# Node-number rows made behind the dst-ordered loop of a graph-network kernel, with table rows on ScalarE and clearing stores on three queues

## What is computed

```python
# layer 0: row = src, col = dst
msg_1 = x @ W_m1.T + b_m1
msg_2 = x @ W_m2.T + b_m2
msg_e = edge_attr @ W_me.T + b_me
msg = relu(msg_1[row] + msg_2[col] + msg_e)
msg = relu(msg @ W_net.T + b_net)
agg = segment_max(msg, row, num_segments=N_NODES)
agg = where(isfinite(agg), agg, 0.0)
x = layernorm(x + x @ W_o1.T + b_o1 + (agg @ W_o2.T + b_o2))
# layer 1
message = mlp2(concat(x[src], x[dst]))
aggregated = segment_sum(message, dst, num_segments=N_NODES)
x = layernorm(x + x + mlp2(concat(x, aggregated)))
```

## Time and profile before

| what | us |
| --- | --- |
| median of 3 runs | 2929.59 |
| the 3 runs | 2926.2, 2930.57, 2929.59 |
| time of the profiled execution | 2931.22 |
| its span | 2929.5 |
| mean granted TensorE clock | 0.942 of full |
| preparation block and sort test | 0 to 174.3 |
| dst-ordered loop block | 174.3 to 1274.6 |
| src-ordered loop block | 1274.6 to 1770.5 |
| node update, second edge loop, output | 1770.5 to 2929.5 |
| busy in the span: TensorE, VectorE, ScalarE, GpSimd | 2376.6, 2027.2, 1025.1, 1903.4 |

### The profile page before, as it was taken

How to read it: one execution, slowest core, us unless ns; L and a number is a source line. 1 busy time by engine, 2 the same in 40 slices (tenths; PEclk the granted TensorE clock), 3 DMA queues, 4 the chain that set the end, 5 groups by cost and what they waited for, 6 DMA issues and landing times. The chain is left out here.

```text
span 2929.5 us, 92861 instructions
## 1 busy us (share of the span) xinstructions
PE 2376.6 (81%) x22750; PEld 2069.7 (71%) x22751; DVE 2027.2 (69%) x10493; ACT 1025.1 (35%) x2315; POOL 1903.4 (65%) x2609
## 2 busy tenths in 40 slices
PE   7857777666677677759999998688888889898997
PEld 6546666555566566647777775588888888898987
DVE  7868988888888888747878776544454555555556
ACT  6324433333333333324444446322222222222225
POOL 1027777777777777754444446677777777777774
PEclk9778988999988989879999999999999999999998
DMA  5112222222222222248898883222222222222221
GB/s 181 40 39 48 47 47 47 47 47 47 47 46 47 47 46 47 65 133 226 226 226 227 226 224 81 52 53 52 52 52 52 52 52 52 52 52 52 52 50 45
DMA packets 603553, 240.09 MB, mean 82 GB/s; under 512 B 533568, under 2 KB 574300, under 8 KB 603228
## 3 DMA queue, kind: packets, MB, share of 16 engines
q1 hardware_dynamic: 439104, 96.80, 16.7%
q0 software_dynamic: 53216, 94.66, 11.6%
q10 hardware_dynamic: 111164, 47.81, 5.8%
HBM read 143.61 MB, written 101.41 MB: 84 GB/s over the span
## 5 line engine op out<-in xcount | busy, mean ns | idle before, releaser
L1000 POOL DMA_INDIRECT edge_in_src_order<-u,place x832 | 808.2, 971 | 275.8 <-issue 212.3
L1555 POOL DMA_INDIRECT a_rows<-src_table,idx x782 | 751.8, 961 | 255.4 <-issue 238.0
L1654 ACT ACTIVATE h<-ps_h 128x512 f32<-128x512 f32 x208 | 124.2, 597 | 773.4 <-PE ps_h L1626 699.7
L1159 PE MATMUL ps_u<-we_s,attrT 128*128 128x384 f32 x416 | 194.6, 551 | 246.8 <-ACT u L1187 246.0
L1254 POOL COPY m_s<-m 128x144 f32 x832 | 233.8, 326 | 245.1 <-PE ps_pre L1301 244.3
L1599 DVE TENSOR_SCALAR ohd_f<-iota_b,dloc_c 128x128 f32<-128x128 bf16 x832 | 184.0, 289 | 280.6 <-PE ps_n L1636 280.4
L1635 PE MATMUL ps_s<-ohd_f,h 128*128 128x128 f32 x1664 | 359.2, 305 | 0.0
L1588 DVE TENSOR_TENSOR hsumT<-hsumT,ps_s 128x128 f32 x832 | 239.0, 287 | 158.3 <-issue 69.9
L1621 PE MATMUL ps_h<-a_rows,ident 128*128 x1664 | 240.6, 288 | 126.2 <-SPq L1564 125.4
L1277 DVE TENSOR_TENSOR_SCAN top<-same,top,ps_net 96x512 f32<-96x512 bf16 x207 | 264.1, 1276 | 98.0 <-PE ps_net L1308 97.7
L1187 ACT COPY u<-ps_u 128x384 f32<-128x384 f32 x208 | 99.7, 479 | 587.8 <-DMA edge_in_src_order<-u,place 564.1
(11 more groups left out here) (309 smaller groups left out, 5497.4 us busy)
## 6 DMA issues: line engine op xcount, KB each, us to landing
u_in<-edge_in_src_order SPq DMA_DIRECT2D x208, 192.0 KB, 3.4
running_max<-row ACTq DMA_DIRECT2D x208, 192.0 KB, 4.1
rowt<-src_row SPq DMA_DIRECT2D x208, 130.0 KB, 3.7
key_in<-edge_keys SPq DMA_DIRECT2D x832, 2.0 KB
attr_in<-edge_attributes SPq DMA_DIRECT2D x832, 8.0 KB
edge_in_src_order<-u,place POOLq DMA_INDIRECT x832
a_rows<-src_table,idx POOLq DMA_INDIRECT x782
edge_attributes<-in_edge_attr ACTq DMA_DIRECT2D x8, 784.0 KB, 12.4
```

What stands on the lines that cost most here:

```text
L1000: pool.indirect_dma_start(u_d, bass.IndirectOffsetOnAxis(place[:, u, j:j + 1], 0), ur[:, u, j, :], None).then_inc(sent[u], 16)
L1159: m.matmul(ps_u.rearrange("p j f -> p (j f)"), attrT[:, u, :], we_s[:].rearrange("p j f -> p (j f)"), start=True, stop=False, skip_group_c ...
L1555: pool.indirect_dma_start(a_rows[:, 4 * u + j, :], None, a_d, bass.IndirectOffsetOnAxis(idx[:, u % 4, j:j + 1], 0)).then_inc(got[u % 4], 16)
```

## The change

In the preparation block:
- the 8 attribute copies move from ScalarE's queue to SP's, behind a wait for the x loads and ahead of the 51 zero stores
- the ten table instructions L556 to L561 (five for each half) move from VectorE to ScalarE, as `activation` with `Copy`; TensorE waits for `rows_read` where it waited for VectorE
- the marks, the sums and the store of the node-number rows are taken out; eight small counts are kept in `begun`, and `at_f`, `iota_w`, `one_w` and `tri` live on
- of the 49 zero stores by block, SP keeps 16, ScalarE's queue gets 16, and 17 move to GpSimd's queue at the start of the next block

In the dst-ordered block:
- GpSimd issues its 17 zero stores, waits for all 49, and only then begins to send
- the attribute loads of groups 0 to 3 are issued by ScalarE's queue, their key loads by SP's
- the output weights are loaded by SP behind its loop, and GpSimd adds the identity to one of them behind its sends
- the marks, sums, rows and their store stand behind the loop on TensorE and VectorE, ahead of the tail

```diff
 # preparation, SP
+                        sp.wait_ge(xt_in, 16 * NT)
+                        part = EP // 8
+                        for c in range(8):
+                            sp.dma_start(attr_d[part * c:part * c + part, :], edge_attr[part * c:part * c + part, :]).then_inc(attr_out, 16)
                         sp.wait_ge(consts, ALL_CONSTS)
...
-                        for b in range(0, NB, 4):
+                        for b in range(0, 16, 4):
...
-                        sp.wait_ge(rows_set, 8)
...
+                        sp.wait_ge(attr_out, 16 * 8)
                         sp.wait_ge(key_out, 16)
 # preparation, ScalarE
-                        act.wait_ge(xt_in, 16 * NT)
...
+                        def row(to, of, scale, bias):
+                            return s.activation(to, of, ACT.Copy, scale=float(scale), bias=float(bias))
+                        for h in range(2):
+                            part = slice(h * HN, (h + 1) * HN)
+                            act.wait_ge(to_dve, 3 + 2 * h)
+                            row(e0_row[:, part], ps_b[0:1, 0:HN], KEY, E * KEY).then_inc(rows_read, 1)
+                            act.wait_ge(to_dve, 4 + 2 * h)
+                            row(db_row[:, part], ps_c[0:1, 0:HN], 1, -1)
...
+                            row(off_s[:, part], ps_c[:, 0:HN], P, -P).then_inc(rows_read, 1)
+                        act.wait_ge(zeros_out, 16 * (NS - FULL + 2))
+                        act.wait_ge(pads_ready, 1)
+                        slots = u_d.rearrange("e f -> (e f)")
+                        for b in range(16, 32, 4):
+                            at = offsets(nc, mybir.EngineType.Activation, pl_row[0:1, b:b + 4], (POS - P) * F)
...
 # preparation, TensorE
-                                pe.wait_ge(to_pe, 5)
+                                pe.wait_ge(rows_read, 2)
...
 # dst-ordered block, SP
+                            if isinstance(i, int) and i < 4:
+                                return
...
                         pipeline(sp, G, [(0, load)])
+                        for to, of in ((wo1_s[:], wo1), (wo2_s[0:F, :], wo2), (wo2_s[F:F + 2, :], bo),
...
+                        sp.wait_ge(rows_set, 8)
 # dst-ordered block, GpSimd
-                        pool.wait_ge(node_w_in, 16 * 6)
...
+                        for b in range(32, NB, 4):
+                            at = offsets(nc, mybir.EngineType.Pool, pl_row[0:1, b:min(b + 4, NB)], (POS - P) * F)
+                            for j in range(min(4, NB - b)):
+                                nc.gpsimd.dma_start(slots[bass.ds(at[j], P * F)].rearrange("(p f) -> p f", f=F), zero_rows[:]).then_inc(rest_set, 16)
+                        pool.wait_ge(pads_set, 16 * 32)
+                        pool.wait_ge(rest_set, 16 * (NB - 32))
+                        pipeline(pool, G, [(0, send)])
+                        pool.wait_ge(node_w_in, 16 * 6)
...
 # dst-ordered block, VectorE, behind the loop and ahead of the tail
+                        for b in range(NB):
+                            wait(dve, marked, b - 3)
+                            v.tensor_scalar(oh_group[:, b % 4, :], iota_w[:, 0:G], at_f[:, 0, b:b + 1], None, ALU.is_equal)
+                            v.tensor_scalar(oh_slot[:, b % 4, :], iota_w[:], at_f[:, 1, b:b + 1], None, ALU.is_equal).then_inc(marks_set, 1)
...
 # dst-ordered block, TensorE, behind the loop
+                        pe.wait_ge(place_chain, 4 * G)
+                        for b in range(NB):
+                            pe.wait_ge(marks_set, b + 1)
...
 # dst-ordered block, ScalarE
+                        act.wait_ge(ones_set, 2)
+                        for i in range(4):
+                            at = offsets(nc, mybir.EngineType.Activation, e0_row[0:1, 4 * i:4 * i + 4], E * KEY)
+                            for j in range(4):
+                                act.dma_start(attr[:, i, j, 1:1 + KA], attrs[bass.ds(at[j] * (KA // KEY), P * KA)].rearrange("(p w) -> p w", w=KA)).then_inc(rec_in[i], 16)
                         pipeline(act, G, [(4, rows), (1, turned)])
```

More of the change, by code:

```diff
@@ L187, in gnn @@
         upto_f = sb(whole, "upto_f", [P, CG])
+        tri = sb(whole, "tri", [P, P])
+        iota_w = sb(whole, "iota_w", [P, 512], F16)
+        at_f = sb(whole, "at_f", [P, 2, HB])
+        one_w = sb(whole, "one_w", [P, 512])
+        begun = sb(whole, "begun", [P, 2, 4])
         e0_row = sb(whole, "e0_row", [1, NS], I32)
@@ L462, in _ @@
                             act.dma_start(we_s[W * j + 1:W * j + 1 + KA, j, :], w_e).then_inc(rows_in, 16)
-                        act.wait_ge(xt_in, 16 * NT)
-                        part = EP // 8
-                        for c in range(8):
-                            act.dma_start(attr_d[part * c:part * c + part, :], edge_attr[part * c:part * c + part, :]).then_inc(attr_out, 16)
                         for b in range(NT):
@@ L548, in _ @@
                         groups(LATE + 8, LATE + 13)
-                        for h in range(2):
-                            if h == 1:
-                                groups(LATE + 13, LATE + 16)
-                            part = slice(h * HN, (h + 1) * HN)
-                            dve.wait_ge(to_dve, 3 + 2 * h)
-                            v.tensor_scalar(e0_row[:, part], ps_b[0:1, 0:HN], float(E), float(KEY), ALU.add, ALU.mult).then_inc(to_pe, 1)
-                            dve.wait_ge(to_dve, 4 + 2 * h)
-                            v.tensor_scalar(db_row[:, part], ps_c[0:1, 0:HN], -1.0, None, ALU.add)
-                            v.tensor_scalar(df_row[:, part], ps_c[0:1, 0:HN], float(F), -float(F), ALU.mult, ALU.add)
-                            v.tensor_scalar(dd_row[:, part], ps_c[0:1, 0:HN], float(D), -float(D), ALU.mult, ALU.add)
-                            v.tensor_scalar(off_s[:, part], ps_c[:, 0:HN], float(P), -float(P), ALU.mult, ALU.add).then_inc(to_pe, 1)
+                        groups(LATE + 13, LATE + 16)
                         groups(LATE + 16, Q8)
@@ L889, in _ @@
                             pe.wait_ge(totals, 1)
-                            m.matmul(ps_first[:, 0:1], tri[:], cum[:, P - 1:P], start=True, stop=True).then_inc(firsts, 1)
+                            m.matmul(ps_first[:, 0:1], tri_s[:], cum[:, P - 1:P], start=True, stop=True).then_inc(firsts, 1)
                             def rank(q, u, n):
@@ L1166, in _ @@
                         pipeline(pe, G, [(2, equal), (1, turn), (3, product), (3, count)])
+                        pe.wait_ge(place_chain, 4 * G)
+                        for b in range(NB):
+                            pe.wait_ge(marks_set, b + 1)
+                            for q, (lo, hi) in enumerate(halves):
+                                mm = m.matmul(ps_mark[q][0:hi - lo, :], oh_group[:, b % 4, lo:hi], oh_slot[:, b % 4, :],
+                                              start=(b == 0), stop=(b == NB - 1), skip_group_check=True)
+                            mm.then_inc(marked, 1)
+                        pe.wait_ge(passed_set, 2)
+                        rest_n = G - P
+                        m.matmul(ps_ahead[:, 0:1], tri[:], passed_c[:, 0, 511:512], start=True, stop=True)
+                        m.matmul(ps_ahead[0:rest_n, 1:2], onesf[:, 0:rest_n], passed_c[:, 0, 511:512], start=True, stop=False)
+                        m.matmul(ps_ahead[0:rest_n, 1:2], tri[0:rest_n, 0:rest_n], passed_c[0:rest_n, 1, 511:512],
+                                 start=False, stop=True).then_inc(ahead_ready, 1)
                         pe.wait_ge(upto_ready, 1)
```

123 lines of the change are left out of this document (59 added, 64 removed).

## The result

The changed kernel takes 2875.6 us (median of four, 2872.1 to 2877.0) against 2928.7 for the kernel before beside it: 0.982, interval 0.980 to 0.983. The profiled execution takes 2875.9 (span 2874.3, where before had 2929.5). The forecast was 2902.0 with a range of 2892 to 2913. So the change brings 53 us where I expected 27.6, and the time lies outside the range on the faster side. The sign is as forecast, and so are most steps. Of what came beyond the forecast, two thirds lie in two loops for which the sum had no term at all.

A forecast was written before the change was run, and what follows sets the result against it. The prediction took the dst-ordered loop to be paced by GpSimd's queue of sends. Its terms, -6.5 - 1.1 - 27 - 1 + 8 = -27.6 us, gave 2902.0 for the median, range 2892 to 2913.

The forecast's parts named there:

- Attribute copies: Preparation: with the copies off ScalarE's queue, ScalarE goes on sooner and TensorE's step comes 5.4 us earlier; -6.5 us.
- Table rows: Preparation: ten rows moved to ScalarE let TensorE do the last five groups of counts without waiting; -1.1 us.
- End of the preparation: Preparation's end: fewer stores on SP, and marks and rows gone, let SP drain at 141.3 instead of 169.2; -27 us.
- Start of the loop: Dst-ordered block's start: two load queues help, but GpSimd's 17 stores nearly use that up; -1 us, ends -5.6 and +2.
- Sends at an unchanged pace: Dst-ordered loop: GpSimd's queue paces it, so only the first send's start moves its end; no term for the pace.
- T does not move against the sends: Dst-ordered loop's end: T, the time of VectorE's last place, keeps its distance to the sends; no term.
- End of the loop: Behind the dst-ordered loop: marks, scans, sums, rows and tail put the next block at T + 36.6, not T + 29.5; +8 us.
- Dear stores on GpSimd: Rival, loop's start: direct stores cost far more than sends and delay the loop; 2967 at 5 us each; 4 in 100.
- A limit shared by SP and ScalarE: Rival, preparation: 32 stores take 19.8 us, not 9.9, so the preparation ends 9.9 later; 2912; 8 in 100.
- Sends starved beside the marks: Rival, loop's end: no send gets through until the marks end, +23.5 instead of +8; 2917.5; 5 in 100.
- A low clock in the marks: Rival, loop's end: TensorE's clock stays low, so the marks take 16 us more; 2918; 4 in 100.
- That the time stays: Rival, whole kernel: the loop's end eats all the gain, time within 0.2% (5.9 us) of before; 3 in 100.

The follow-up runs named there:

- e8: Changed kernel with the ten table rows back on VectorE; key store to first block store 26.97 us, ratio to the kernel before 0.995 (0.990 to 0.999).
- e12: Changed kernel with the first four groups' attribute loads back on SP's queue; block to first send 27.4 us, where the changed kernel has 22.3.
- e10: Kernel before with only GpSimd's weight wait and one addition moved behind the sends; ratio 0.994 (0.988 to 0.999).

## Why the prediction was right or wrong

- **Attribute copies, right.** -6.45 at the key store, -6.5 forecast, and 0.45 more behind `pl_row`. TensorE's step comes 5.3 us earlier (30.48, before 35.81) and its wait ahead of it is 3.68 us where it was 6.88: shorter, but not gone or under 2 as I had it. The granted clock from 35 to 40 is 1.00, the higher level, where it was 0.50.

```profile
30.48 0.58 PE L639 MATMUL ps_m<-m,nidentb 128*128 128x480 bf16 x1 [3.68 <-ACT m L432]
```

```profile
35.00:40.00 5.00, 4.75 (x63) 4.02 (x62) 3.64 (x10) 3.24 (x8) 0.00 (x0) 1.00 0.66 173
```

- **Table rows, right in size.** 1.3 to 1.7 by e8, 1.1 forecast. The whole gain between key store and first block store is 2.05; 1.60 of it lies ahead of `pl_row` and 0.45 behind it.
- **End of the preparation, a little short.** -37.1 up to the block against -34.6. Last store to block is 5.0, and the stores start 8.5 earlier: from `pl_row` to SP's first store it is 0.99 us, where before had 1.44, and 16 stores took 9.57, not 9.9. The price of ScalarE's queue, for which no row stood, was SP's (9.65 for 16).
- **Start of the loop, the mis-sized term.** I priced a direct store on GpSimd's queue like an indirect one, 1.27 us, since that row was on the same queue. It is 0.54 (the first two 0.80 and 0.57), and 17 with their loads of addresses took 11.5 us (138.98 to 150.44), not 25. They end 9.1 us before the first send, so they cost nothing, and what moved the first send is the loads on two queues (e12). By the other end of my bound the term was -5.6; it measured -5.0. The Trainium skill, "DMA: Bandwidth & Descriptors", section "Anatomy of one DMA — SWDGE (gpsimd) path", which I weighed, spoke for that end, and the trace agrees: 0.54 us on the queue, 2.2 to landing. I let the indirect send speak against it, though its 0.97 us is another kind of work.
- **Sends at an unchanged pace, the step that failed.** "T does not move against the sends" held, but the sends moved: 10 ns each, and 11 for the gathers of a loop that the change doesn't touch. "Everything behind must be as long as before" was 1655 us of span without a term and without a bound. It was 8.6 shorter, and the first loop 10.0: 18.6 of the 27.7 us that the forecast missed. Without them the time would have been 2894, inside the range. What the runs showed in the step's place: a transfer's duration on GpSimd's queue isn't fixed. The change also moved one addition from right ahead of the sends to behind them, a move that I took for free, and e10 shows that this alone brings 958 and 944 ns. A bound of 6 ns either way on each of the 1614 transfers would have been 10 us on each side of the range.
- **End of the loop, right in mechanism.** T + 35.0 against T + 37.5: 0.9 for a late rise of the clock wasn't needed, and scans, sums and rows took 5.8, not 6.5, the tail 4.4, not 4.9. GpSimd's drain is over 3.4 us before VectorE's, which is last, as forecast.
- **The rivals.** Dear stores on GpSimd: no, 0.54 each and at most 0.80. A limit shared by SP and ScalarE: no, both at 0.60. Sends starved beside the marks (which are comparisons, not copies as I wrote): no; ten of fourteen took 0.10 longer, 1.0 us in all, hidden. The Trainium skill's rule ("SBUF — State Buffer", section "Who interferes with whom") would have them wait for whole instructions of VectorE, which are 0.26 and 0.34 us here; the trace shows 0.10 at most and none for the first four, and nothing was held up until the marks' end. A low clock in the marks: no, the 98 matmuls took 23.9 us. That the time stays: no.
- **Left over:** +2.1 in the output and -1.8 in the src-ordered loop and node update aren't explained; no run was made for them.

## What to carry to other kernels

When two engines hold the end of a block, removing the one that isn't last shows nothing (0 us here), and removing the last shows only the distance to the next (9.3 of 30.6): look for all that end late before you price one. A queue that paces a loop of hundreds of equal instructions multiplies a few ns by their number, so put a bound on the pace itself in the sum, and compare the median duration of that instruction first when a result is off. Work moved behind a loop is free only while another engine still has its backlog, and the backlog can differ between chips: GpSimd's last send starts 18.5 us behind T on the first chip and 4.9 to 9.0 on the others. And before you blame an instruction for what comes behind it, look whether the same step is already there ahead of it.

## What the hardware showed

- GpSimd issues a direct store of 128 rows in 0.54 us (the first in 0.80), and a group of four with its loads of addresses in 2.7, against 0.96 for an indirect one and 1.26 from start to start.
- Indirect transfers of GpSimd took 971, 967, 962 or 958 ns in the median for the same work. An addition right ahead of the loop of sends is worth 9 ns on these and 11 on the gathers behind; another 3 to 4 ns belong to the whole execution, seen in GpSimd's instructions from 2 us on, and what sets them is open.
- SP and ScalarE, issuing stores at the same time, take 0.60 us a store each, no more than SP alone (0.618).
- GpSimd's drain after the sends takes 8.56 us in both kernels.
- Of fourteen sends beside VectorE's comparisons in 16-bit tiles, the last ten took 1.06 instead of 0.96 us, and the first four did not.
